# Graph network on one core: ScalarE issues its 40 parameter loads ahead of its part in the first layer norm instead of behind it

## What is computed

```python
edge_index = jnp.stack([src, dst])
h = jnp.maximum(_layernorm(x, axis=-1), 0.0)
x = x + _L0_gnn_ref(h, edge_index, W1, a_src1, a_dst1, b1, W2, a_src2, a_dst2, b2)   # attention, twice
h = jnp.maximum(_layernorm(x, axis=-1), 0.0)
x = x + _L1_gnn_ref(h, edge_weight, weights, src, dst)                               # Lanczos
...
# in the attention layer:
h = (x @ W).reshape(-1, H, C)
al_src = jnp.einsum('nhc,hc->nh', h, a_s)
al_dst = jnp.einsum('nhc,hc->nh', h, a_d)
e = jax.nn.leaky_relu(al_src[src] + al_dst[dst], NEG_SLOPE)
```

## Time and profile before

| | us |
|---|---|
| median of three runs | 6127.14 |
| lowest, highest of them | 6108.68, 6155.19 |
| the profiled execution | 6163.28 |
| its span, first to last instruction | 6161.6 |
| mean granted TensorE clock in it | 0.681 |

### The profile page before, as it was taken

The page is one execution under the profiler, slowest core; times in us unless marked ns, Lnnn a source line. Parts: engine busy times, 40 slices in busy tenths (PEclk is TensorE's granted clock), DMA queues, the critical chain, the costliest instruction groups (busy, mean ns, idle before and its releaser), DMA issues.

```text
span 6161.6 us, 57827 instructions
## 1 busy us (share of the span) xinstructions
PE 3246.0 (53%) x17251; PEld 1781.1 (29%) x17252; DVE 3418.0 (55%) x3986; ACT 1742.3 (28%) x2404; POOL 3654.0 (59%) x2519
## 2 busy tenths in 40 slices
PE   1322222222214557775336878699999934444444
PEld 0222122112111222222332222244445413333333
DVE  5576767766757989996997898611210051111111
ACT  0000000000003448896444888600111050000001
POOL 0277777777777889898887885000000007777774
PEclk6555555555557878898555887899999965555555
DMA  9422222222228963333995333377567642222222
GB/s 410 135 1 1 1 1 1 1 1 1 1 1 279 349 203 96 99 87 112 315 307 158 94 99 79 109 280 277 205 232 256 230 169 52 52 52 52 52 52 41
DMA packets 445355, 760.76 MB, mean 123 GB/s; under 512 B 273431, under 2 KB 351449, under 8 KB 405461
## 3 DMA queue, kind: packets, MB, share of 16 engines
q1 hardware_dynamic: 275280, 702.23, 33.4%
q0 software_dynamic: 163840, 54.71, 9.6%
q10 hardware_dynamic: 6146, 2.68, 0.2%
HBM read 552.67 MB, written 187.47 MB: 120 GB/s over the span
## 4 chain that ended last, share of the span: by engine, by line
PE 24%; issue 20%; POOL 19%; DVE 14%; DMA 12%; ACT 3%; SPq 1%; POOLq 1%; DVEq 0%; ACTq 0%
PE PS L647 20%; POOL edge_weight_and_count L590 14%; POOL tiles L621 6%; DVE tiles L1509 5%; DVE feature_major L1455 4%; DMA tiles<-edge_weight_and_count 4%; DMA edge_weight_and_count<-weight_and_count,target 3%; DVE tiles L1502 3%; DMA copies_then_records<-edge_count 2%; DMA tiles<-message_table,gather_index 2%; PE PS L840 1%; PE PS L769 1%; PE PS L958 1%; DMA message_table<-tiles 1%; ACT copies_then_records L1083 1%
## 5 line engine op out<-in xcount | busy, mean ns | idle before, releaser
L621 POOL DMA_INDIRECT tiles<-message_table,gather_index x808 | 775.7, 960 | 1531.1 <-DMA message_table<-tiles 1285.2
L610 POOL DMA_INDIRECT sorted_edges<-record_slot,place_slot x784 | 1507.4, 1923 | 271.5 <-issue 225.1
L590 POOL DMA_INDIRECT edge_weight_and_count<-weight_and_count,target x784 | 1242.0, 1584 | 624.5 <-issue 256.1
L647 PE MATMUL PS<-tiles 128*64 128x392 f32 (+1 forms) x3200 | 741.7, 592 | 248.2 <-DVE tiles L1509 244.5
L691 PE MATMUL PS<-consts,key_slot 128*128 128x128 f32 x798 | 197.2, 425 | 1200.3 <-DVE target L1339 1196.8
L647 PE MATMUL PS<-tiles,node_major 128*128 128x448 f32 (+1 forms) x2100 | 811.1, 546 | 11.1 <-ACT node_major L1014 10.8
L958 PE MATMUL PS<-tiles 128*128 128x128 f32 x1616 | 491.8, 460 | 614.4 <-DMA tiles<-message_table,gather_index 614.4
L1509 DVE SCALAR_TENSOR_TENSOR tiles<-tiles,copies_then_records 128x1568 f32<-128x1568 f32 (+1 forms) x400 | 704.6, 1794 | 99.7 <-ACT tiles L1117 86.1
L1455 DVE SCALAR_TENSOR_TENSOR feature_major<-tiles,s,feature_major 128x1600 f32<-128x1600 f32 (+3 forms) x384 | 679.6, 1851 | 40.4 <-ACT tiles L1070 40.3
L1656 DVE TENSOR_TENSOR tiles<-lane_row,edges 128x1024 f32<-128x1024 f32 x101 | 123.6, 1225 | 882.0 <-PE PS L958 872.1
L958 PEld LDWEIGHTS PS<-tiles 128*128 128x128 f32 x1616 | 374.8, 322 | 731.9 <-issue 731.9
(11 more groups left out here) (246 smaller groups left out, 3036.3 us busy)
## 6 DMA issues: line engine op xcount, KB each, us to landing
tiles<-edge_weight_turned SPq DMA_DIRECT2D x72, 1568.0 KB, 7.4
tiles<-edge_count SPq DMA_DIRECT2D x72, 1568.0 KB, 7.0
tiles<-edge_weight_and_count SPq DMA_DIRECT2D x48, 1600.0 KB, 8.8
edge_weight_and_count<-feature_major SPq DMA_DIRECT2D x48, 1568.0 KB, 39.3
copies_then_records<-edge_count SPq DMA_DIRECT2D x192, 392.0 KB
tiles<-edge_weight_and_count SPq DMA_DIRECT2D x48, 1536.0 KB
edge_weight_turned<-copies_then_records SPq DMA_DIRECT2D x48, 768.0 KB, 4.8
edge_count<-copies_then_records SPq DMA_DIRECT2D x24, 800.0 KB, 4.6
```

The source lines that it names most:

```text
L590: nc.gpsimd.indirect_dma_start(out=edge_d, out_offset=bass.IndirectOffsetOnAxis(ap=idx[:, s, a:a + 1], axis=0), in_=pay[:, s, a, :], in_of ...
L610: nc.gpsimd.indirect_dma_start(out=rec_d, out_offset=bass.IndirectOffsetOnAxis(ap=place_slot[:, s, a:a + 1], axis=0), in_=rec_slot[:, s, a ...
L621: nc.gpsimd.indirect_dma_start(out=msg[:, s, a, :], out_offset=None, in_=table_d, in_offset=bass.IndirectOffsetOnAxis(ap=gs[:, s, a:a + 1] ...
L647: return nc.tensor.matmul(out_ap, lhsT, rhs, start=start, stop=stop)
```

## The change

The wait for `consts_made` and ScalarE's part of the first layer norm move from between the edge loads and the parameter loads to behind the parameter loads. Nothing is added or removed. All 40 parameter loads are moved past, the three slopes and the last three small ones too.

```diff
--- before.py
+++ after.py
@@ -1022,8 +1022,6 @@
                 for k, a in enumerate((src, dst, etype)):
                     act.dma_start(edges[part, k, 0:n], a[rng].rearrange("(p c) -> p c", c=n)).then_inc(S("edges_loaded"), 16)
                 act.dma_start(wF[part, 0:n], eweight[rng].rearrange("(p c) -> p c", c=n)).then_inc(S("edges_loaded"), 16)
-            act.wait_ge(S("consts_made"), 1)
-            layer_norm(0)
             for n, a in loads:
                 act.dma_start(mat(n), a).then_inc(S("params"), 16)
             for n, a in vec:
@@ -1034,6 +1032,8 @@
             act.dma_start(msge[:, :], msgW[:, D:D + 32]).then_inc(S("params"), 16)
             act.dma_start(msgb_row[:, :], msgb.rearrange("(o p) -> o p", o=1)).then_inc(S("params"), 16)
             act.dma_start(emb[:, :], embW).then_inc(S("params"), 16)
+            act.wait_ge(S("consts_made"), 1)
+            layer_norm(0)
             for layer in range(2):
                 for b in range(CH):
                     act.wait_ge(S("gat_h"), CH * layer + b + 1)
```

## The result

| | before | after |
|---|---|---|
| median of 20 runs each, us | 6127.66 | 6166.36 |
| lowest, highest, us | 6108.43, 6182.75 | 6119.4, 6200.93 |
| the profiled execution's span, us | 6161.6 | 6151.9 |
| start of the first scatter in it, us | 257.65 | 286.59 |

The ratio of after to before is 1.0045, with a 95% interval of 1.0027 to 1.0064: the change costs about 28 us (17 to 39). The medians themselves lie 39 us apart; the runs of each kernel spread over 74 and 82 us. The two profiled executions stand the other way round by 9.7 us. That does not come from the head of the program, which is where the change is; where it does come from is told further down, with rival 3.

What follows compares the result with a forecast made beforehand. The head before GpSimd's first scatter was taken to bound: the 50 products 28.3 us later plus 0.7 for TensorE's clock, +29 us on 6127, gives 6156, range 6124 to 6194; within 1%: 0.92.

Steps and rivals of the forecast that it cites:

- rival 3: After the head: the scatter stage waits for something else later, so 29 us of lateness costs nothing; 6127; chance 0.04.
- The head bounds, and a late first scatter goes through one for one: Head of some 250 us before GpSimd's first scatter: a shift of that scatter goes to the end one for one.
- The loads go 20 us earlier: ScalarE's queue q10: loads issued behind the edges, last landing 20 us sooner, at 172.4; alone worth 20 us.
- ScalarE's issues are held and hold the layer norm: ScalarE: 40 issues wait for queue room, last ends at 140.4 (127 to 160.4); first layer norm ends 111.5 us later.
- Rival 1: ScalarE: issues take 0.5 us each and do not hold the layer norm up; -20 us, 6107; chance 0.07.
- rival 2: ScalarE: the issues end no earlier than now, at 160.4; +49 us, 6176; chance 0.07.
- The sum behind it: Behind the last issue: layer norm, VectorE's 72.3 us preparation, selectors; TensorE's 50 small products start at 229.5, +28.3 us.
- TensorE's clock: TensorE's 50 small products, after some 35 us idle, run at a lower clock: +0.7 us, at most +1.65.
- The advice to issue early: Trainium skill's rule to issue DMAs early and compute behind them; by it the change would be the gain of Rival 1.

Runs made afterwards that it cites:

- nine ahead: Against the kernel before: 9 of the 40 parameter loads issued ahead of ScalarE's layer norm, 31 behind it; ratio 0.9967, first scatter 237.28 us.
- 24 ahead: Against the kernel before: 24 of the 40 parameter loads issued ahead of ScalarE's layer norm, 16 behind it; ratio 0.997, first scatter 236.09 us.
- the three below them in the table: Against the kernel before: 40 loads ahead, clears behind them, 0.9939; 3 ahead on their own semaphore, 0.9938; 3 ahead, 37 on SP behind the clears, 0.991.
- 32 ahead: Against the kernel before: 32 of the 40 parameter loads issued ahead of ScalarE's layer norm, 8 behind it; one run, no ratio, first scatter 258.22 us.

## Why the prediction was right, point by point

**The head bounds, and a late first scatter goes through one for one.** The first scatter starts at 257.65 and 286.59, the last one at 1876.2 and 1904.9 (the rows of line 590, first and last start). 28.9 us in, 28.7 out. It holds in the other kernels too: the last scatter lies 21.7 us ahead of that before with nine and with 24 ahead, 36.7, 47.1 and 53.4 ahead in the three below them in the table, and 0.3 behind with 32 ahead.

```profile
L590 POOL DMA_INDIRECT edge_weight_and_count<-weight_and_count,target x784: 1557/1561/3081, 257.7 to 1876.2; - x196
```

```profile
L590 POOL DMA_INDIRECT edge_weight_and_count<-weight_and_count,target x784: 1557/1561/3079, 286.6 to 1904.9; - x196
```

(The first is of the kernel before, the second of the changed one.)

**The loads go 20 us earlier.** Right, and isolated by nine ahead: -20.4 us.

**ScalarE's issues are held and hold the layer norm.** Last issue said at 140.4 (bounds 127 and 160.4), measured 138.9. The cause is shown: with no clears beside them the same 40 issues end at 28.6. The way there was not quite as I had it: the first issue to be held was the seventh (3.55 us at 10.68), not the tenth. Rival 1 falls with the 139.0 us of waiting, rival 2 with 138.9 instead of 160.4.

**The sum behind it.** Layer norm from ScalarE's start to VectorE's end: said 16.3, measured 154.50 - 138.98 = 15.5; TensorE ran the variances in 6.96 us, faster than the 8.12 of the product at 192.41 from which I had taken them. Preparation 72.3 said, 154.50 to 226.99 = 72.5 to the selectors. Together: the 50 products start +26.3 us instead of +28.3.

**TensorE's clock** is the term that was mis-sized. I took +0.7, at most +1.65; it is 10.72 - 7.75 = +3.0, beyond what I had called the most. The windows of those 50 products in the changed kernel (busy us of PE, PEld, DVE, ACT, POOL, then the granted clock):

```profile
227.60:232.00 4.40, 4.40 (x21) 4.40 (x21) 0.00 (x0) 0.00 (x0) 0.00 (x0) 0.50 0.02 4
232.00:238.20 6.20, 6.20 (x31) 6.17 (x30) 0.00 (x0) 0.00 (x0) 0.00 (x0) 0.50 0.00 0
```

The clock is 0.50, the 1.2 GHz level, from start to end, after 39 us without work, and a product takes 0.214 us (10.72 / 50) where I had 0.188 from the low end of the earlier trace rows. That was a misreading: a window counts the products at its edges as well, these two count 52 of 50, so the 16 in 3.00 us are about 14 products' worth. The same 10.7 us was measured in each of the four other kernels in which the 50 products come after 21 to 71 us without work. With nine ahead, where they follow the attention product closely as in the kernel before, VectorE waits for them as long as it did then, 16.16 and 16.15 us. The two errors, -2.0 and +2.3 us, nearly cancel (what follows them moved by -0.4). That the head came out at the 29 us said is in this part luck; with either error alone it would have been 27 or 31, still within the range.

**Rival 3, the delay is taken up later,** is what the two profiled executions seem to say: 6161.6 and 6151.9. They do not. The 28 us are there at the end of the scatters and again at the start of the attention stage: ScalarE's exponentials run from 2279.2 in the one and 2307.2 in the other. What differs comes later, above all in the second attention round, here about 3310 to 3960 us in the kernel before and 3340 to 3960 in the changed one (busy us of the five engines, the granted clock, DMA):

```profile
3310.00:3960.00 650.00, 501.66 (x2010) 141.84 (x2010) 552.82 (x429) 525.52 (x626) 418.66 (x193) 0.79 0.35 94
```

```profile
3340.00:3960.00 620.00, 436.11 (x2025) 131.88 (x2026) 561.11 (x451) 528.75 (x633) 459.30 (x179) 0.91 0.39 102
```

About the same 2010 and 2025 matmuls took 501.66 us of TensorE at a mean granted clock of 0.79 and 436.11 us at 0.91. From its first exponential to its last the second round took 601.8 us (3326.4 to 3928.2) in the kernel before and 562.7 (3361.8 to 3924.5) in the changed one, 39.1 us less; the first round took 569.3 and 576.8, 7.5 us more, and what comes behind both 6.0 us less. With the 28.0 this gives the -9.7. The other six traces say that it is the clock: over the 16 rounds of the eight kernels, all of the same work, the length goes from 562.7 us at a mean granted clock of 0.93 to 603.7 at 0.82, while the stretch between the two rounds stays within 473.4 and 477.9 us.

A draw of the clock in one stage is larger than the change, which is why a pair of profiles can't give its price and the ratio over 20 runs can. The same draw spreads the other runs, as the mean clock recorded with each says: of the changed kernel's 20 the fastest (6119.4) had 0.697 and the slowest (6200.93) 0.676. It is also why the profiled execution took 6153.7 us where I had said about 6192: I had let it stand 0.6% above the median as the one before did. What draws the clock, no run shows.

**The advice to issue early.** The Trainium skill, DMA: Bandwidth & Descriptors, Rules for kernel authors, advises to issue a DMA early and compute behind it; in its section Issuing engines are not separate DMA queues the issue itself counts as usually small beside the DMA. With room in the queue the trace agrees (0.45 us each, with the clears out of the way), and an early issue of nine loads gave its 20 us. Beside the clears neither holds once the queue is full, from the tenth load on in the kernel before and from the seventh in the changed one, where edges are still queued: most issues cost 3.3 to 3.4 us and some about 10, as long as the loads themselves are served (3.7 us each), and they stand in the stream of the engine that is to compute behind them.

## What to carry to other kernels

Before moving DMA issues ahead of an engine's work, read in the trace how long issues take at the time to which they move, and not how long the shortest one takes. Where a bulk transfer keeps the DMA engines full, as here, each issue behind the first six to nine costs as long as a load is served, 3.7 us on average, and all that the engine owes behind it waits, at every place to which the issues are put. Count then how much of the delay the others' slack covers (here all of it with 24 of the 40 loads ahead; with 32 the gain of the early loads was spent, with 40 there was a loss), and put ahead only what the next step reads, the rest on an engine that owes nothing. A single profile of each kernel can have the opposite sign to the change, if a stage elsewhere draws its clock.

## What was not expected of the hardware

The issues are not held evenly. Beside the clears most take 3.3 to 3.4 us, but once every eight or nine, some 31 us apart, there are a pair of 0.48 and about 10 us (18.89 us: 10.55; 50.62: 10.24; 82.03: 10.00; 112.46: 9.86 in the changed kernel), at the times when SP's issue takes 5 to 7 us. SP has such an issue in the kernel before too, while ScalarE issues nothing (16.52 us: 6.07). No run here shows what this beat is; the sums only need its mean, 3.7 us for a load.

```profile
18.38 0.48 ACTq L1026 DMA_DIRECT2D consts<-in_L_gnn_Wself_dram  x1
18.89 10.55 ACTq L1026 DMA_DIRECT2D consts<-in_L_gnn_Wneigh_dram  x1
...
50.10 0.48 ACTq L1029 DMA_DIRECT2D columns<-in_L_gnn_a_src_dram  x1
50.62 10.24 ACTq L1029 DMA_DIRECT2D columns<-in_L_gnn_a_dst_dram  x1
```

And a load of 512 bytes, spread as 4 bytes on each of 128 partitions, holds the issue as long as one of 64 KB (3.41 us at 60.89, a vector; 3.41 at 46.66, a matrix, in the changed kernel): both have one row per partition, and beside the clears packets go one for one. In the kernel before, issuing the 21 vectors and slopes took from 70.2 to 152.3 us, issuing the 16 matrices from 40.8 to 70.1.
